# The expert stage of a fused embedding, attention and routed FFN kernel: rows of 64 experts by 2 units, gates loaded twice, gelu in place in PSUM

## The chip, the cores and the metric

The program runs on one core of a Trainium2 chip. The metric is the device time of one execution in microseconds (us). The engines are TensorE (PE; its weight loads are PEld), VectorE (DVE), ScalarE (ACT), GpSimd (POOL) and SyncE (SP, which here only issues DMAs). Each takes its own queue in order; semaphores tie them.

## What is computed

64 images give 16 patch tokens and 77 text tokens each, 5952 tokens of 192 numbers. After an attention of its own kind comes the part that the change is about, for each of S=8 subspaces of R=16 numbers, with M=64 experts of H=32 hidden units and the best K=4 chosen:

```
z = einsum('nd,sdr->nsr', layernorm(h), P)
scores = einsum('nsr,smr->nsm', z, C);  topv, topi = top_k(scores, 4);  w = softmax(topv)
hid = gelu(einsum('nsr,nskrh->nskh', z, W1[s,topi]) + b1[s,topi])      # tanh form
comb = einsum('nskr,nsk->nsr', einsum('nskh,nskhr->nskr', hid, W2[s,topi]) + b2[s,topi], w)
h = h + gelu(comb @ G1 + g1b) @ G2 + g2b
```

## The kernel before

Three stages follow each other. The **first** (to about 141 us) embeds: PE multiplies one-hots with the text tables and the patches with their matrix, POOL gathers word rows, DVE normalizes, SP stores the text rows (`store_text`, L426). Beside it W1 is split into three bf16 parts, W2 is placed into `w2p` by ACT, and each part of b2 into `b2p`.

The **second** (to about 858 us) goes through 16 units of 372 tokens with attention (a), its second half (b) and router (g) of three units interleaved in one pass (`pass_pe`, `pass_dve`, `pass_act`, `pass_pool`). It ends with the gates of all 512 experts for each token, zero where an expert isn't chosen, transposed by PE into PSUM. They are split into three bf16 parts: ACT casts (`gate_part1`), DVE subtracts (`rest`, L1143), ACT casts the rest (`gate_part2`), POOL subtracts again (`gate_part3`, L662). SP stores the three parts to DRAM. PE makes the product of gates and b2 (`bias`), ACT copies it.

The **third**, the expert stage, doesn't gather weights: it computes all experts for 12 tiles of TN=496 tokens and multiplies the hidden values by the gates. A tile has 8 blocks of 4 quads, 32 quads; a quad has 4 chunks k of 128 rows, each 16 experts by 8 units in a row of products. Its steps are `hidden` (PE, two bf16 products of 496 columns into one of two PSUM pairs, twice a quad), gelu of a pair by ACT into `hid` in SBUF (L936), `spread` (PE: the gates of 16 experts, spread over 128 rows by the 0/1 matrix `sel`, into one of two PSUM banks, L1561), the multiply of the whole quad by DVE into `gated` (L1326, 1984 elements), and `decode` (PE: 4 fp32 products into the four 32-row groups of one bank, summed over the tile, L1573). `gated` holds two blocks; `decode(block, k)` reads chunk k of all four quads of a block and runs one block later. POOL takes every eighth quad (`POOL_QUADS`, L740) from a copy of the gates that ACT makes. After a tile ACT copies the sum (L946), POOL adds the bias, and PE, ACT and DVE do G1, gelu, G2 and the last add (L1581, L950, L1589, L1338) inside the next tile. The order in each queue is written out by hand: `tile_pe` issues per quad the next spread, a hidden pair two quads ahead (`AHEAD` = 4 pairs), a decode, and another hidden pair. SP reloads gates and codes of the next tile by quarters (`refill`) and starts each tile with a load of the bias (L523).

## Time and profile before

| | |
|---|---|
| Time, median of 3 runs | 1804.54 us (1804.47 to 1810.88) |
| Span of the profiled execution | 1811.7 us |
| PE busy in the span | 1622.6 us (90%) |
| DVE, ACT, POOL busy | 1351.4, 1095.4, 718.0 us |
| First stage, to the last text store | about 141 us |
| Second stage, to the first expert gelu | about 717 us |
| Expert stage to its last decode | about 936 us, 12 tiles |

The times are those of whole executions; the span of the profiled one is 7.2 us over their median. Busy times overlap, so they don't add up to the span. A timeline row is an instruction, or some of the same kind merged (x), with its start and its length. What stands in brackets is the idle time of the engine before it, and what ended that. The records of matmuls overlap, since a matmul drains while the next one streams: the distance of two starts says what one costs in the queue, not its length.

### The profile page before, as it was taken

The page shows a single profiled execution, that of the slowest core. Times are in us where ns is not written, and L with a number is a line of the kernel's source. Part 1 is how long each engine was busy: PE and PEld are TensorE (multiplying, and loading weights), DVE is VectorE, ACT ScalarE, POOL GpSimd, SP SyncE. Part 2 cuts the span into 40 slices and gives each one's busy share as a digit, 9 for nine tenths or more (in the row PEclk, how much of TensorE's full clock was granted, in tenths as well). Part 3 has the DMA queues.
Part 4 walks back from the last instruction along what each step waited for, and adds up shares of the span by engine and source line. Part 5 has one row for each costly group of instructions (what it writes and reads, how often), then busy time and mean ns, then how long its engine had stood idle before and what let it go on. Part 6 is the DMA issues. An engine that isn't in the chain of part 4 may idle for free.

```text
span 1811.7 us, 31074 instructions
## 1 busy us (share of the span) xinstructions
PE 1622.6 (90%) x8824; PEld 674.4 (37%) x8824; DVE 1351.4 (75%) x2824; ACT 1095.4 (60%) x2122; POOL 718.0 (40%) x656
## 2 busy tenths in 40 slices
PE   5974888888888888874999999999999999999997
PEld 3631665555666665661122222222222212222221
DVE  4471488878888878875878877878878878878874
ACT  0131244545444445522888888888888888888884
POOL 4460366656666666663222222222222222222221
PEclk9755899989999999985899999999999999999998
DMA  7337012112112221114211121212212121121200
GB/s 225 99 92 85 22 42 80 57 55 65 55 55 58 72 77 56 58 50 112 51 26 43 38 51 25 66 32 48 49 25 56 30 56 40 39 51 25 66 24 9
DMA packets 120652, 102.38 MB, mean 57 GB/s; under 512 B 16951, under 2 KB 117743, under 8 KB 120175
## 3 DMA queue, kind: packets, MB, share of 16 engines
q1 hardware_dynamic: 117097, 94.99, 21.1%
q0 software_dynamic: 2112, 3.79, 0.8%
q10 hardware_dynamic: 1376, 2.88, 0.5%
q8 instruction: 21, 0.34, 0.1%
q14 instruction: 46, 0.38, 0.1%
HBM read 58.74 MB, written 39.62 MB: 54 GB/s over the span
## 4 chain that ended last, share of the span: by engine, by line
PE 73%; DVE 13%; issue 5%; POOL 3%; ACT 3%; DMA 2%; SPq 0%; DVEq 0%; POOLq 0%; ACTq 0%
PE pair L1546 22%; PE bank L1573 20%; PE bank L1561 6%; PE bank L1478 4%; PE pair L1447 4%; DVE arena L1118 3%; PE pair L1458 3%; PE pair L1417 2%; PE pair L1416 2%; DVE arena L1098 2%; PE bank L1366 2%; DVE arena L1107 2%; DVE arena L1201 1%; PE bank L1589 1%; PE bank L1440 1%
## 5 line engine op out<-in xcount | busy, mean ns | idle before, releaser
L1326 DVE TENSOR_TENSOR arena<-arena,bank 128x1984 f32<-128x1984 f32 x336 | 734.1, 2218 | 176.2 <-ACT arena L936 162.1
L936 ACT ACTIVATE arena<-pair 128x992 f32<-128x992 f32 x768 | 739.0, 998 | 156.7 <-PE pair L1546 156.7
L740 POOL TENSOR_TENSOR arena<-arena 128x992 f32<-128x992 f32 x96 | 219.1, 2304 | 698.0 <-PE bank L1573 685.0
L1546 PE MATMUL pair<-arena,w_stack 99*128 99x496 bf16 x1536 | 459.5, 382 | 13.6 <-ACT arena L936 13.6
L1573 PE MATMUL bank<-arena,w_pad 128*32 128x496 f32 x3072 | 399.0, 592 | 1.2 <-DVE arena L1326 1.2
L1546 PEld LDWEIGHTS pair<-arena,w_stack 99*128 99x128 bf16 x1536 | 88.1, 97 | 412.0 <-ACT arena L936 311.5
L1561 PE MATMUL bank<-arena,sel 48*128 48x496 bf16 x384 | 147.0, 383 | 0.6 <-ACT arena L838 0.6
L1573 PEld LDWEIGHTS bank<-arena,w_pad 128*32 128x32 f32 x3072 | 60.8, 108 | 160.4 <-issue 158.3
L1458 PE MATMUL pair<-arena 128*128 128x94 f32 x768 | 110.2, 306 | 2.6 <-DVE arena L1165 2.4
L1478 PE MATMUL bank<-arena 128*124 128x192 f32 x576 | 106.9, 337 | 3.7 <-POOL arena L675 3.7
L1458 PEld LDWEIGHTS pair<-arena 128*128 128x128 f32 x768 | 106.6, 222 | 3.3 <-DVE arena L1165 2.6
L667 POOL TENSOR_TENSOR arena<-arena 128x372 f32<-128x372 f32 x96 | 92.1, 974 | 33.1 <-DVE arena L1170 32.9
L1447 PE MATMUL pair<-arena 128*32 128x93 f32 x768 | 69.6, 302 | 36.8 <-DVE arena L1201 36.8
L1478 PEld LDWEIGHTS bank<-arena 128*124 128x124 f32 x576 | 94.4, 190 | 11.4 <-issue 5.5
L1561 PEld LDWEIGHTS bank<-arena,sel 48*128 48x128 bf16 x384 | 35.4, 92 | 161.2 <-issue 148.4
L1403 PE MATMUL bank<-ident,arena 124*128 124x124 f32 x96 | 25.0, 294 | 76.3 <-DVE arena L1098 76.3
L831 ACT ACTIVATE arena<-pair 128x93 f32<-128x93 f32 x384 | 91.4, 271 | 0.0
L1417 PE MATMUL pair<-arena 64*128 64x372 f32 x192 | 90.9, 556 | 0.0
L1416 PE MATMUL pair<-arena 128*128 128x372 f32 x192 | 86.9, 536 | 1.3 <-ACT arena L823 1.0
L822 ACT COPY arena<-bank 128x372 f32<-128x372 f32 x32 | 15.0, 468 | 116.9 <-PE bank L1404 116.9
L831 ACT ACTIVATION_READ_ACCUMULATOR arena<-pair 128x1 f32 x384 | 85.1, 230 | 0.0
L675 POOL TENSOR_TENSOR arena<-arena 128x372 f32<-128x372 f32 x96 | 81.1, 865 | 5.1 <-DVE arena L1188 5.1
(141 smaller groups left out, 1929.0 us busy)
## 6 DMA issues: line engine op xcount, KB each, us to landing
gate_parts<-arena SPq DMA_DIRECT2D x48, 372.0 KB, 6.7
arena<-gate_parts SPq DMA_DIRECT2D x576, 31.0 KB, 1.8
arena<-h_scratch SPq DMA_DIRECT2D x32, 279.0 KB
arena<-z_parts SPq DMA_DIRECT2D x144, 62.0 KB, 2.2
h_scratch<-arena SPq DMA_DIRECT2D x16, 279.0 KB
z_parts<-arena SPq DMA_DIRECT2D x48, 93.0 KB, 1.7
arena<-h_scratch SPq DMA_DIRECT2D x12, 372.0 KB
out_h<-arena SPq DMA_DIRECT2D x12, 372.0 KB
```

Source lines behind the costliest of these rows:

```text
L740: p_.tensor_tensor(gated[:, block % 2, j, pair], hid[:, quad % 4, pair], gcopy.unsqueeze(1).to_broadcast([128, 2, TN]), ALU.mult).then_inc ...
L831: last = a_.activation(wsq[:, c, N * b:N * b + N], src[:, N * b:N * b + N], ACT.Square, accum_out=n2[:, c, b:b + 1])
L936: a_.activation(hid[:, quad % 4, 2 * (pair % 2):2 * (pair % 2) + 2], (pair0, pair1)[pair % 2][:, :, 0:TN], ACT.Gelu_apprx_tanh).then_inc(s ...
L1326: v_.tensor_tensor(gated[:, block % 2, j], hid[:, quad % 4], gate_banks[quad % 2][:, 0:TN].unsqueeze(1).to_broadcast([128, KH, TN]), ALU.m ...
L1416: t_.matmul(o, wq0[:, 128 * c:128 * c + 128], xt0["A"], start=True, stop=False)
L1417: t_.matmul(o, wq1[:, 128 * c:128 * c + 128], xt1["A"], start=False, stop=True).then_inc(s_wp, 1)
L1447: last = t_.matmul(pair1[32 * b:32 * b + 32, 0, 0:N], lsel[:, b, c], wsq[:, c, N * b:N * b + N], start=(c == 0), stop=(c == CH - 1))
L1458: last = t_.matmul(pair0[:, c % 2, (N + 1) * b:(N + 1) * (b + 1)], headsel[:, b, c], pi, start=True, stop=True)
L1478: last = t_.matmul(o, wpi[:, c, ST * s:ST * s + ST], wout[:, c], start=(c == 0), stop=(c == CH - 1))
L1546: mm = t_.matmul((pair0, pair1)[pair % 2][:, a, 0:TN], w1s[:, x:x + 128], zst[:, o, j], start=True, stop=True)
L1561: t_.matmul(gate_banks[quad % 2][:, 0:TN], sel[rows], gst[rows, block, j // 2], start=True, stop=True).then_inc(s_gb, 1)
L1573: mm = t_.matmul(code_bank[32 * j:32 * j + 32, 0:TN], w2p[:, chunk(2 * j + o, eb, k)], gated[:, block % 2, j, k], start=(block == 0 and k ...
```

## The change

A product row of the expert stage holds 64 experts by 2 units instead of 16 by 8. A quad is split into two **duos** of two chunks, 64 duos per tile; a quad covers the 64 experts of one subspace with 8 of their units, a duo with 4 of them. So the 128 gate rows that multiply it are the 64 gates loaded twice, into partitions 0 to 63 and 64 to 127 of `gst` (fp32), straight from DRAM. `spread`, `sel` and its banks go; the two banks become `pair2`, the third PSUM pair of a ring. ACT's gelu of a duo writes back into its pair, and DVE multiplies from PSUM (992 elements, 42 duos of a tile). The 22 duos of `POOL_DUOS` have their gelu written into SBUF, where POOL multiplies them. A hidden product waits until the previous user of its pair is multiplied (or, for a POOL duo, until its gelu is done). The gates are kept in fp32 only, so in the second stage `gate_part2`, `gate_part3` and `rest` go and one copy stays; b2 is placed once in fp32 and `bias` has 4 products instead of 24. The weights are regrouped to the new rows: W2 comes in 32 small loads that SP issues after the last image product (`sp.wait_ge(s_ips, 8)`), between text stores 2 and 3; b1 in 8 loads; W1's casts and ACT's placing are cut into four and eight instructions.

```diff
-POOL_QUADS = [q for q in range(QUADS) if q % 8 == 4]
-DVE_QUADS = QUADS - len(POOL_QUADS)
+DUOS = 2 * QUADS
+POOL_DUOS = [d for d in range(DUOS) if d % 11 in (2, 5, 8, 10) and d != 32]
+DVE_DUOS = DUOS - len(POOL_DUOS)
+RING = [d % 3 for d in range(DUOS - 4)] + [0, 1, 0, 2]
 AHEAD = 4
+BIAS_AFTER = 10
...
+def dve_gated(tile, duo):
+
+    return DVE_DUOS * tile + sum(d not in POOL_DUOS for d in range(duo + 1))
+
+
+def pool_gated(tile, duo):
+
+    return len(POOL_DUOS) * tile + sum(d <= duo for d in POOL_DUOS)
+
+
+def same_buffer_before(tile, duo):
+
+    for d in range(duo - 1, -1, -1):
+        if RING[d] == RING[duo]:
+            return tile, d
+    return tile - 1, max(d for d in range(DUOS) if RING[d] == RING[duo])
+
+
+def first_of_half_block(duo, mine):
+
+    return not any(d in mine for d in range(duo - duo % 8 + duo % 2, duo, 2))
...
-        banks = [ctx.enter_context(nc.psum_tensor(f"bank{i}", [128, 512], F32)) for i in range(2)]
+        pair2 = ctx.enter_context(nc.psum_tensor("pair2", [128, 2, 512], F32))
+        banks = [pair2[:, 0], pair2[:, 1]]
...
-        gst = c3(128, [8, 2, TN], BF16)
+        gst = c3(128, [2, PAIRS, TN])
         zst = c3(ZROWS, [2, PAIRS, TN], BF16)
         assert c3.at <= attended_end
-        hid = c3(128, [4, KH, TN])
+        hid = c3(128, [2, 2, TN])
...
+            sp.wait_ge(s_ips, 8)
+            w2_from = t["w2"].rearrange("(m g a) (s e x) -> a e g m s x", m=16, a=2, s=S, e=EB)
+            for a in range(2):
+                for e in range(EB):
+                    for g in range(EB):
+                        rows = slice(64 * a + 16 * e, 64 * a + 16 * e + 16)
+                        sp.dma_start(w2f[rows, g], w2_from[a, e, g]).then_inc(s_w2f, 16)
...
-            def load_gates(tile, q):
-                for p in range(3):
-                    for a in range(2):
-                        for b in range(2):
-                            r = 64 * a + 16 * p
-                            sp.dma_start(gst[r:r + 16, 2 * q + b],
-                                         gq_r[p, a, q // 2, q % 2, b, :, :, bass.ds(tile * TN, TN)]
-                                         ).then_inc(s_gl[q], 16)
+            def load_gates(tile, o):
+                for h in range(2):
+                    sp.dma_start(gst[64 * h:64 * h + 64, o],
+                                 gq_r[o, :, :, bass.ds(tile * TN, TN)]).then_inc(s_gl[o], 16)
...
-                wait_apart(sp, (s_gb, QUADS * (tile - 1) + 8 * (q + 1)),
-                           (s_hp1, 2 * QUADS * (tile - 1) + 16 * (q + 1)))
-                load_gates(tile, q)
-                if q % 2 == 1:
-
-                    load_codes(tile, q // 2)
+            def refill(tile, o):
+
+
+                wait_apart(sp, (s_hp1, DUOS * (tile - 1) + DUOS // 2 * (o + 1)))
+                load_codes(tile, o)
+                last = DUOS // 2 * (o + 1) - 1
+                wait_apart(sp, (s_gat, dve_gated(tile - 1, last)), (s_pg, pool_gated(tile - 1, last)))
+                load_gates(tile, o)
...
-                if has(g - 1):
-                    gate_part3(g - 1, 2)
...
+            def gate_duo(tile, duo):
+
+                quad, a = divmod(duo, 2)
                 block, j = divmod(quad, PAIRS)
-                wait(pool, s_code, QUADS * tile + PAIRS * (block - 1))
-                pool.wait_ge(s_gc, pool_quads(tile, quad))
-                pool.wait_ge(s_hid, 2 * QUADS * tile + 2 * quad + 2)
-                for half in range(2):
-                    pair = slice(2 * half, 2 * half + 2)
-                    p_.tensor_tensor(gated[:, block % 2, j, pair], hid[:, quad % 4, pair],
-                                     gcopy.unsqueeze(1).to_broadcast([128, 2, TN]), ALU.mult).then_inc(s_pg, 1)
+                if duo == first_pool[block // EB]:
+                    pool.wait_ge(s_gl[block // EB], 32 * (tile + 1))
+                if first_of_half_block(duo, POOL_DUOS):
+                    wait(pool, s_code, QUADS * tile + PAIRS * (block - 2) + 2 * a + 2)
+                pool.wait_ge(s_hid, DUOS * tile + duo + 1)
+                p_.tensor_tensor(gated[:, block % 2, j, 2 * a:2 * a + 2], hid[:, POOL_DUOS.index(duo) % 2],
+                                 gst[:, block // EB, j].unsqueeze(1).to_broadcast([128, 2, TN]),
+                                 ALU.mult).then_inc(s_pg, 1)
...
+            def gates_copy(u, s):
                 act.wait_ge(s_gt, SUB * u + s + 1)
                 if s == 0:
-                    wait(act, s_gd, 48 * u)
+                    wait(act, s_gd, 16 * u)
                     wait(act, s_bp, u)
-                a_.copy(gh[:, 0, :, ST * s:ST * s + ST],
-                        gt_bank(s)[:, 0:4 * ST].rearrange("p (a b) -> p a b", a=4)).then_inc(s_g1, 1)
-
-            def gate_part2(u, s):
-                act.wait_ge(s_grr, SUB * u + s + 1)
-                a_.copy(gh[:, 1, :, ST * s:ST * s + ST], grr[:, s]).then_inc(s_g2, 1)
+                a_.copy(gh[:, :, ST * s:ST * s + ST],
+                        gt_bank(s)[:, 0:4 * ST].rearrange("p (a b) -> p a b", a=4)).then_inc(s_gc, 1)
...
+            def gelu(tile, duo):
+
+                act.wait_ge(s_hp1, DUOS * tile + duo + 1)
+                product = ring[RING[duo]][:, :, 0:TN]
+                if duo in POOL_DUOS:
+                    wait(act, s_pg, pool_gated(tile, duo) - 2)
+                    a_.activation(hid[:, POOL_DUOS.index(duo) % 2], product, ACT.Gelu_apprx_tanh).then_inc(s_hid, 1)
+                else:
+                    a_.activation(product, product, ACT.Gelu_apprx_tanh).then_inc(s_hid, 1)
...
-                if has(g - 1):
-                    rest(g - 1, 2)
...
+            dve_duos = [d for d in range(DUOS) if d not in POOL_DUOS]
+            first_dve = [min(d for d in dve_duos if d >= DUOS // 2 * o) for o in range(2)]
+
+            def gate_duo(tile, duo):
+                quad, a = divmod(duo, 2)
                 block, j = divmod(quad, PAIRS)
-                if j == 0 or quad - 1 in POOL_QUADS:
-                    wait(dve, s_code, QUADS * tile + PAIRS * (block - 1))
-                v_.tensor_tensor(gated[:, block % 2, j], hid[:, quad % 4],
-                                 gate_banks[quad % 2][:, 0:TN].unsqueeze(1).to_broadcast([128, KH, TN]),
+                if duo == first_dve[block // EB]:
+                    dve.wait_ge(s_gl[block // EB], 32 * (tile + 1))
+                if first_of_half_block(duo, dve_duos):
+                    wait(dve, s_code, QUADS * tile + PAIRS * (block - 2) + 2 * a + 2)
+                dve.wait_ge(s_hid, DUOS * tile + duo + 1)
+                v_.tensor_tensor(gated[:, block % 2, j, 2 * a:2 * a + 2], ring[RING[duo]][:, :, 0:TN],
+                                 gst[:, block // EB, j].unsqueeze(1).to_broadcast([128, 2, TN]),
                                  ALU.mult).then_inc(s_gat, 1)
...
-                for i in range(6):
-                    for j in range(PAIRS):
-                        mm = t_.matmul(pair1[32 * j:32 * j + 32, 0, 0:UT], b2p[:, j, WP[i]], gh[:, ZP[i], j],
-                                       start=(i == 0), stop=(i == 5), skip_group_check=True)
+                for j in range(PAIRS):
+                    mm = t_.matmul(pair1[32 * j:32 * j + 32, 0, 0:UT], b2p[:, j], gh[:, j], start=True, stop=True)
...
-            def hidden(tile, pair):
-
-                block, j = divmod(pair // 2, PAIRS)
-                o, eb = divmod(block, EB)
-                if pair % QUADS == 0:
+            def hidden(tile, duo):
+
+                quad, a = divmod(duo, 2)
+                block, j = divmod(quad, PAIRS)
+                o, hb = divmod(block, EB)
+                if duo % (DUOS // 2) == 0:
                     pe.wait_ge(s_zl[o], 96 * (tile + 1))
-                wait(pe, s_hid, 2 * QUADS * tile + pair - 1)
-                for a in range(2):
-                    x = chunk(2 * j + o, eb, 2 * (pair % 2) + a) * 128
-                    mm = t_.matmul((pair0, pair1)[pair % 2][:, a, 0:TN], w1s[:, x:x + 128], zst[:, o, j],
+                before = same_buffer_before(tile, duo)
+                if before[1] in POOL_DUOS:
+                    wait(pe, s_hid, DUOS * before[0] + before[1] + 1)
+                else:
+                    wait(pe, s_gat, dve_gated(*before))
+                for k in range(2):
+                    x = chunk(2 * j + o, hb, 2 * a + k) * 128
+                    mm = t_.matmul(ring[RING[duo]][:, k, 0:TN], w1s[:, x:x + 128], zst[:, o, j],
                                    start=True, stop=True)
                 mm.then_inc(s_hp1, 1)
 
-            def spread(tile, quad):
-
-                block, j = divmod(quad, PAIRS)
-                if quad % (QUADS // 4) == 0:
-                    pe.wait_ge(s_gl[block // 2], 192 * (tile + 1))
-                before = (tile, quad - 2) if quad >= 2 else (tile - 1, quad - 2 + QUADS)
-                if before[1] in POOL_QUADS:
-                    pe.wait_ge(s_gc, pool_quads(*before))
-                else:
-                    wait(pe, s_gat, dve_gated(*before))
-                rows = slice(64 * (j % 2), 64 * (j % 2) + 48)
-                t_.matmul(gate_banks[quad % 2][:, 0:TN], sel[rows], gst[rows, block, j // 2],
-                          start=True, stop=True).then_inc(s_gb, 1)
-
             def decode(tile, block, k):
 
-                if k == 0:
-                    pe.wait_ge(s_gat, dve_gated(tile, PAIRS * block + PAIRS - 1))
-                    wait(pe, s_pg, 2 * pool_quads(tile, PAIRS * block + PAIRS - 1))
-                    if block == 0:
-                        wait(pe, s_comb, tile)
+                if k % 2 == 0:
+                    needed = 2 * (PAIRS * block + PAIRS - 1) + k // 2
+                    pe.wait_ge(s_gat, dve_gated(tile, needed))
+                    pe.wait_ge(s_pg, pool_gated(tile, needed))
+                if k == 0 and block == 0:
+                    wait(pe, s_comb, tile)
...
                 for quad in range(QUADS):
-                    spread_next(quad)
                     hidden_ahead(quad, AHEAD)
+                    hidden_ahead(quad, AHEAD + 1)
                     decode_next(quad)
-                    hidden_ahead(quad, AHEAD + 1)
```

PE inside a tile, around the output product of the tile before. In the rows `pair` is a hidden product, `sel` a spread, `w_pad` a decode. Before:

```order
L1573 MATMUL bank<-arena,w_pad 32x496 x4
L1546 MATMUL pair<-arena,w_stack 128x496 [waits hidden_gelu]
L1546 MATMUL pair<-arena,w_stack 128x496
L1561 MATMUL bank<-arena,sel 128x496 [waits hidden_gated]
L1546 MATMUL pair<-arena,w_stack 128x496 [waits hidden_gelu]
L1546 MATMUL pair<-arena,w_stack 128x496
L1573 MATMUL bank<-arena,w_pad 32x496 [waits hidden_gated_by_pool,hidden_gated]
L1573 MATMUL bank<-arena,w_pad 32x496 x3
L1546 MATMUL pair<-arena,w_stack 128x496 [waits hidden_gelu]
L1546 MATMUL pair<-arena,w_stack 128x496
L1561 MATMUL bank<-arena,sel 128x496 [waits gates_copied]
```

After, from decode k=3 of block 0 to decode k=0 of block 1 (register rows compute what is waited for):

```order
L1528 MATMUL bank<-arena,w_pad 32x496 x4
L83 REGISTER_ALU
L1514 MATMUL pair<-arena,w_stack 128x496 [waits hidden_gated]
L1514 MATMUL pair<-arena,w_stack 128x496
L83 REGISTER_ALU
L1514 MATMUL pair<-arena,w_stack 128x496 [waits hidden_gated]
L1514 MATMUL pair<-arena,w_stack 128x496
L1523 REGISTER_ALU [waits hidden_gated]
L1528 MATMUL bank<-arena,w_pad 32x496 [waits hidden_gated_by_pool]
L1528 MATMUL bank<-arena,w_pad 32x496 x3
```

The spread is gone, both hidden products of a quad stand ahead of its decode, and they wait for a multiply (`hidden_gated`) where they waited for a gelu.

DVE, first tile of the expert stage, the multiplies before (`chunk_decoded` is the semaphore of the decodes):

```order
L1326 TENSOR_TENSOR arena<-arena,bank 128x1984 [waits bias_stored,gates_stored,hidden_gelu,z_stored,gates_spread,h1_stored,w1_stack_written]
L1326 TENSOR_TENSOR arena<-arena,bank 128x1984 [waits gates_spread,hidden_gelu] x6
L1326 TENSOR_TENSOR arena<-arena,bank 128x1984 [waits chunk_decoded,gates_spread,hidden_gelu]
L1326 TENSOR_TENSOR arena<-arena,bank 128x1984 [waits gates_spread,hidden_gelu] x3
L1326 TENSOR_TENSOR arena<-arena,bank 128x1984 [waits chunk_decoded,gates_spread,hidden_gelu]
L1326 TENSOR_TENSOR arena<-arena,bank 128x1984 [waits gates_spread,hidden_gelu] x2
```

And after:

```order
L1291 TENSOR_TENSOR arena<-pair,arena 128x992 [waits bias_stored,gates_stored,gates_loaded0,z_stored,hidden_gelu,h1_stored,w1_stack_written]
L1291 TENSOR_TENSOR arena<-pair,arena 128x992 [waits hidden_gelu] x10
L1291 TENSOR_TENSOR arena<-pair,arena 128x992 [waits hidden_gelu,chunk_decoded] x2
L1291 TENSOR_TENSOR arena<-pair,arena 128x992 [waits hidden_gelu] x3
L1291 TENSOR_TENSOR arena<-pair,arena 128x992 [waits hidden_gelu,chunk_decoded] x2
L1291 TENSOR_TENSOR arena<-pair,arena 128x992 [waits hidden_gelu] x3
```

The twelfth and thirteenth multiply (duos 17 and 18) wait for decodes of two blocks before; 16, 19 and 21 are POOL's.

POOL in a pass of the second stage, before:

```order
L635 TENSOR_SCALAR arena<-arena 124x3 [waits normed_G,moments_G]
L637 TENSOR_TENSOR arena<-arena 124x3 [waits var_eps_G]
L667 TENSOR_TENSOR arena<-arena 128x372 [waits w_pi] x2
L662 TENSOR_TENSOR arena<-arena 128x4x124 [waits gate_part2]
L667 TENSOR_TENSOR arena<-arena 128x372 [waits w_pi] x4
L641 TENSOR_TENSOR arena<-arena 128x372 [waits z_part1]
```

And after:

```order
L647 TENSOR_SCALAR arena<-arena 124x3 [waits normed_G,moments_G]
L649 TENSOR_TENSOR arena<-arena 124x3 [waits var_eps_G]
L674 TENSOR_TENSOR arena<-arena 128x372 [waits w_pi] x6
L653 TENSOR_TENSOR arena<-arena 128x372 [waits z_part1]
```

The residue of the gates (L662) that stood behind the first two products with `w_pi` is gone.

## Rows read from the trace of the kernel before

**Rows 1.** Stretches of the execution: us, busy us of each engine (x instructions), granted clock, DMA share.
```profile
870.00:1750.00 880.00, 871.66 (x4818) 190.07 (x4816) 701.24 (x338) 727.13 (x793) 223.07 (x103) 1.00 0.18 41
588.00:592.00 4.00, 1.91 (x17) 1.91 (x17) 4.00 (x10) 0.83 (x2) 3.35 (x4) 0.97 0.26 78
592.00:596.00 4.00, 4.00 (x12) 2.43 (x12) 2.95 (x9) 0.03 (x1) 2.42 (x3) 0.60 0.57 183
```

**Rows 2.** Costliest groups of the page: busy us, mean ns of one | idle before, releaser.
```profile
L1326 DVE TENSOR_TENSOR arena<-arena,bank 128x1984 f32<-128x1984 f32 x336 | 734.1, 2218 | 176.2 <-ACT arena L936 162.1
L936 ACT ACTIVATE arena<-pair 128x992 f32<-128x992 f32 x768 | 739.0, 998 | 156.7 <-PE pair L1546 156.7
L740 POOL TENSOR_TENSOR arena<-arena 128x992 f32<-128x992 f32 x96 | 219.1, 2304 | 698.0 <-PE bank L1573 685.0
L1546 PE MATMUL pair<-arena,w_stack 99*128 99x496 bf16 x1536 | 459.5, 382 | 13.6 <-ACT arena L936 13.6
L1573 PE MATMUL bank<-arena,w_pad 128*32 128x496 f32 x3072 | 399.0, 592 | 1.2 <-DVE arena L1326 1.2
```

**Rows 3.** Timeline of one quad: start us, us, engine line; all engines.
```profile
1299.97 0.59 PE L1546 MATMUL pair<-arena,w_stack 99*128 99x496 bf16 x2
1300.49 0.38 PE L1561 MATMUL bank<-arena,sel 48*128 48x496 bf16 x1
1300.59 1.91 ACT L936 ACTIVATE arena<-pair 128x992 f32<-128x992 f32 x2 [0.42 <-PE pair L1546]
1301.32 1.04 PE L1573 MATMUL bank<-arena,w_pad 128*32 128x496 f32 x8
1302.30 0.38 PE L1546 MATMUL pair<-arena,w_stack 99*128 99x496 bf16 x1
```

**Rows 4.** Timeline of SP, bias loads of two tiles that follow each other.
```profile
1341.23 0.34 SPq L523 DMA_DIRECT2D arena<-bias_codes  x1
...
1418.91 0.36 SPq L523 DMA_DIRECT2D arena<-bias_codes  x1
```

**Rows 5.** Timeline, end of the expert stage.
```profile
1783.95 6.88 DVE L1326 TENSOR_TENSOR arena<-arena,bank 128x1984 f32<-128x1984 f32 x3 [2.13 <-ACT arena L936]
1790.89 3.53 PE L1573 MATMUL bank<-arena,w_pad 128*32 128x496 f32 x32 [1.23 <-DVE arena L1326]
1794.49 0.57 ACT L946 COPY arena<-bank 128x496 f32<-128x496 f32 x1 [5.91 <-PE bank L1573]
1800.58 0.56 DVE L1338 TENSOR_TENSOR arena<-bank,arena 124x384 f32<-124x384 f32 x1 [9.74 <-PE bank L1589]
```

**Rows 6.** Timeline, a multiply that waited for its gelu.
```profile
1365.20 1.00 ACT L936 ACTIVATE arena<-pair 128x992 f32<-128x992 f32 x1
1366.19 6.48 DVE L1326 TENSOR_TENSOR arena<-arena,bank 128x1984 f32<-128x1984 f32 x3 [1.28 <-ACT arena L936]
```

**Rows 7.** Stage before: POOL's timeline; L1098 in two stretches (ns min/median/max); PE's timeline.
```profile
588.85 1.07 POOL L662 TENSOR_TENSOR arena<-arena 128x496 bf16<-128x496 f32 x1
...
L1098 DVE TENSOR_SCALAR arena<-arena x1: 1115/1115/1115, 588.9 to 588.9; 124x192 f32<-124x192 f32 x1
...
L1098 DVE TENSOR_SCALAR arena<-arena x3: 369/370/882, 580.8 to 581.8; 124x192 f32<-124x192 f32 x3
...
590.09 0.33 PE L1403 MATMUL bank<-ident,arena 124*128 124x124 f32 x1 [2.46 <-DVE arena L1098]
```

**Rows 8.** Timeline of POOL where the expert stage begins.
```profile
848.16 1.06 POOL L662 TENSOR_TENSOR arena<-arena 128x496 bf16<-128x496 f32 x1 [0.76 <-ACT arena L876]
...
856.38 0.50 POOL L730 MEMSET arena<- 1x496 f32 x1 [7.17 <-DMA bias_codes<-arena]
```

**Rows 9.** First stage: ACT's timeline, DVE's timeline, SP's text stores (ns min/median/max).
```profile
84.17 0.32 ACT L768 COPY arena<-bank 128x192 f32<-128x192 f32 x1 [4.03 <-PE bank L1368]
...
105.74 0.94 DVE L1009 TENSOR_TENSOR arena<-arena 112x768 f32<-112x768 f32 x1
...
L426 SPq DMA_DIRECT2D h_scratch<-arena x44: 553/566/832, 40.9 to 138.8; - x44
```

235 lines of the change are left out of this document (80 added, 155 removed).

## The prediction

> **What bounds the kernel now.** I read the busy times by stretch first. In the expert stage PE is busy 871.7 of 880 us at the full clock [rows 1], while ACT is busy 83%, DVE 80% and POOL 25% of it. So it is bound by the matmul queue, with nothing to gain on the others. The period of a tile, from one bias load to the next in SP's timeline, is 77.68 us [rows 4]: twelve such tiles make half of the time. The timeline of one quad [rows 3] shows what fills it: a pair of hidden products takes 0.52 us until the next group starts (1299.97 to 1300.49), the spread product 0.31, the second pair again 0.52 (so it began at 1300.80), four decode products 0.98 (1301.32 to 1302.30), together 2.33. 32 quads are 74.6 us; the remaining 3.1 us of a tile are the output products. ACT waits 0.42 us per quad for PE there.
>
> The stage before (attention, router and gates; 160 to 850 us) is bound by a chain that passes through DVE and PE in turns. One link of it [rows 7]: the third of the normalizations (L1098) takes 1.115 us while POOL does a residue of the gates (L662, 588.85 to 589.92), and PE waits 2.46 us for them; with POOL idle the same instruction takes 0.37 us.
>
> **The change, expert stage: PE's work.** Per quad the spread product goes (0.31), and the two pairs now stand side by side, which saves one more changeover: 0.52 - 0.413 = 0.11. That leaves 2.33 - 0.42 = 1.91 us, and 32 x 1.91 + 3.1 = 64.2 us per tile. If PE stayed the bound, 13.5 us per tile or 162 us in all would be gained. The other engines would allow about that: ACT 64 gelus at 0.91 us from start to start (two in 1.91, the second 1.00, [rows 3]) = 58.2 plus 1.2 for code copy and output gelu; DVE 42 multiplies at 1.10 and two adds = 47; POOL 22 at 2.25 to 2.30 = 51 [rows 2].
>
> **What the ring costs.** A hidden product goes into one of three PSUM pairs, and for 42 of 64 duos the pair is held until DVE has multiplied. Before, a pair was free after its gelu. One turn costs: hidden start to gelu start 0.62 (1299.97 to 1300.59, [rows 3]); gelu 1.00 [rows 2]; gelu end to DVE start 0.00 (1365.20 + 1.00 against 1366.19, [rows 6]); multiply 1.19; DVE end to PE start 0.06 (1783.95 + 6.88 = 1790.83 against 1790.89, [rows 5]). The multiply of 992 elements isn't in the trace: it lies between 0.56 us for 384 elements [rows 5] and 2.22 for 1984 [rows 2], both with one operand in PSUM, so 0.56 + 608 x 1.04 ns = 1.19; consecutive ones overlap by 0.09 (three in 6.48, [rows 6]), so 1.10 from start to start. The turn is 2.87 us for a distance of three duos, where PE needs 0.96 per duo. PE takes its queue in order, and a decode stands behind every two hidden products. So an even duo, its multiply, the odd duo three further, then a decode: 2.87 + 0.52 + 0.98 = 4.37 us for two quads, where PE alone would need 3.82. With a second gelu and multiply in between (+0.91 + 1.10) it is 6.38 for three quads (5.73 alone).
>
> **A second wait, on the gated buffer.** Duo 8b+1 (units 2 and 3 of the block) writes what decode k=3 of block b-2 reads. That decode stands in PE's queue behind hidden 8b+3; hidden 8b+4 needs multiply 8b+1. So in blocks 2 to 4, where 8b+1 and 8b+2 are DVE's: decode start to its semaphore 1.08 (1.04 to the end of its records, [rows 3], and 0.04 for the last step, 0.07 at most between PE's end 1794.42 and the copy at 1794.49, [rows 5]), multiply 1.10, multiply and release 1.25, hidden and changeover 0.52: 3.95 us for one quad instead of 1.91.
>
> **One tile added up** (32 quads, along PE, ACT and DVE in turn): blocks 2 to 4 with the buffer wait 3 x 3.95 + 0.47 for an output add between = 12.3 (3 quads); four two-quad loops 17.5 and 1.7 for output products in them = 19.2 (8); two three-quad loops 12.8 (6); the four quads over the tile's boundary 0.98 + 4.88 + 2.87 + 0.52 = 9.25; duo 1 behind decode k=3 of block 6, 1.08 + 1.25 + 2.87 + 0.52 = 5.7 (2); the code copy, which ACT does before gelu 10 and which waits for the last decode: 1.08 + 0.48 + 0.91 + 1.00 + 1.10 + 1.25 + 0.52 = 6.3 (2); seven quads at 1.91 = 13.4. Sum 78.9 us, 1.25 more than now, with PE idle 15 us of it. **12 tiles: +15 us.**
>
> Bounds of the unknown durations. No row has a gelu that writes PSUM. From below, 0.91 us, its present distance from start to start, gives 77.7 per tile, no change in all; from above, the 1.19 us of DVE's operation of that size out of PSUM gives 82.5, +58. I take the 0.998 of the same gelu into SBUF, the nearest row [rows 2]; a twentieth more, 1.05, would be +24. A multiply of 1.15 or 1.22 gives 78.1 or 79.5, +5 to +22. The POOL multiplies have their row.
>
> On the gelu in PSUM the Trainium skill speaks to both sides ("ScalarE: Activation LUTs", section "Step-by-step: what each stage is for"): an activation into PSUM is faster than into SBUF, with the caveat that this is only of use where TensorE doesn't need most of PSUM. It gives no figure, and no run here yet shows either; by its first half the sum would move toward the lower bound, and the ring above is a case of its caveat.
>
> Ends of the stage. First gelu to last decode is now 1794.4 - 858.4 = 936.0 us, 12 x 77.68 and 3.9 more, part of it slow clock in the first tile. In the new order the first tile has no earlier tile to wait for (-2.8), the slow clock stays (some +4): **-2.5 us.** The gate loads (two for each half of a tile) have half a tile, 39 us, to land, and cost nothing; without that cover the first multiply of a half would wait for all of one landing.
>
> **The stage before.** POOL's residue (48 L662), DVE's subtraction (48 L1143) and ACT's second cast go. DVE's and ACT's lie in slots where the next step waits for another engine, so nothing is taken for them. POOL's third one lies on the link in question [rows 7]: 1.115 - 0.37 = 0.75 us per unit, with 15 of 16 units **-11 us**; what is late next is PE's transposes, that follow at once. Bounds 0 (if POOL's next product slides into the gap) and -13. The bias product gets shorter off the chain. **The hand-over** loses one cast, one subtraction, one residue and most of the bias product of the last unit: POOL ends the residue at 849.22, and the store lands at 856.38 [rows 8]; copied gates would be ready some 3 us earlier, with one larger store: **-3**, bounds -4.5 and 0.
>
> These stretched rows have their rule in the Trainium skill ("SBUF — State Buffer", section "Who interferes with whom"): one port pair is shared by DVE and GpSimd as an exclusive lock, taken by a tensor_scalar in its fast mode and not by a tensor_tensor with a single SBUF input. The trace agrees, 1.115 against 0.37 us, and by the rule the new multiplies with one PSUM input stay free of POOL's 22.
>
> **First stage.** SP now waits for the last image product (its copy is at 84.17, [rows 9]) and then issues 32 small loads of w2, before the store of text step 3. At 0.566 us per issue (L426) that is 18.1 us, to 102.6; the store follows to 104.9 and lands near 107. DVE's step at 105.74 needs it: **+2 us**, bounds 0 and +8 (if small rows land slowly, the gathers and ACT's placing of w2 come late as well). Behind SP's wait stand only these stores.
>
> **Sum.** +15 - 2.5 - 11 - 3 + 2 = +0.5 us on the profiled span of 1811.7, which is 7 us over the median of 1804.5; what lies around the span doesn't change. On the median: **1805 us.** Half a per cent (9 us) is about what a measurement can tell.
>
> **Rivals.**
> *A: the ring doesn't bind.* For it: PE alone needs 64.2, every engine has room. Against: [rows 3, 5, 6] give each link of the turn, and PE's queue is in order. Time 1804.5 - 162 - 12 = 1630. Chance 0.06.
> *B: links are shorter.* Gelu in PSUM at 0.91 us, multiply at 1.15: 76.8 per tile, -10 instead of +15: 1780; half of that 1792. For it: gelus already follow each other at 0.91. Against: the 1.19 interpolates between two rows. Chance 0.23.
> *C: slower, PE's clock falls.* In the stage before, a stretch of 4 us with 1.9 us of PE work is followed by one at 0.60 of the clock [rows 1], between 1.2 and 2.4 GHz. In the new stage PE is idle 15 of 79 us, in pieces up to 1.3 us, instead of 1 in 80. If each tile spends 5 us at the lower clock, 2.5 us are lost: +30, 1835. It decides from one such stretch of 3 us per tile on. Against it: the pieces are short and PE is 80% busy. Chance 0.16.
> *D: the early loads or the unchanged pass eat the gain of the first two stages:* +13 to +19, 1820. Chance 0.13.
> *Forecast* as summed, 1796 to 1813: 0.42.
>
> **Range and chances.** 1780 to 1838 leaves out A and the ends of C. Faster by over 0.5%: A, B = 0.29; within 0.5%: 0.42; slower: C, D = 0.29.
>
> **What would show it.** In the new profile: the tile period 78.9; PE idle near 15 us per tile, waiting for ACT and DVE's multiply; PE waits 1.2 to 1.3 us behind each decode k=3 of blocks 0 to 2, with DVE waiting for PE's decode; gelus at 1.00; multiplies at 1.19; the third L1098 at 0.4 us; text stores held up behind the w2 loads. A period near 64 would prove the ring wrong, a granted clock under 0.98 in the expert stage would be C, a gelu row of 0.9 B.

## The result: slower by 2.2%, 1845 us where 1805 was forecast

| | before | after |
|---|---|---|
| median, us | 1806.8 (1804.5 to 1810.9) | 1845.0 (1839.2 to 1853.0) |
| ratio, 95% interval | | 1.022 (1.018 to 1.026) |
| profiled execution: span, us | 1811.7 | 1851.2 |
| mean granted clock of PE | 0.920 | 0.903 |

Times are medians; one of the four executions of e9 (5431.7 us) and one of e10 (1766.0 us), both slow ones, are left out of theirs. The time lies above the range (1780 to 1838). Split at the first h0 load of the attention stage (SP's first load from `h_scratch`) and at the first gelu of the expert stage, the profiled span grew by +6.4 us in the first stage (forecast +2), by -27.9 in the attention stage with the hand-over (forecast -14), and by +61.5 in the expert stage up to its last decode (forecast +12.5). So the miss of 40 us is, to 1 us, the sum of +49 in the expert stage, +4 in the first and -14 in the attention stage: without that last one the forecast would have been further off.

The expert stage by stretches, kernel after (us, busy us of PE, PEld, DVE, ACT, POOL, granted clock, DMA share); the first line answers to the first of [rows 1], the others are one place of a tile:

```profile
870.00:1750.00 880.00, 737.88 (x4180) 164.25 (x4180) 526.88 (x467) 656.67 (x701) 544.18 (x244) 0.96 0.21 46
...
1286.00:1288.00 2.00, 0.81 (x3) 0.25 (x4) 1.86 (x4) 0.98 (x1) 1.71 (x1) 0.88 0.00 0
1288.00:1290.00 2.00, 2.00 (x10) 0.20 (x8) 1.22 (x2) 0.98 (x1) 0.00 (x0) 0.50 0.00 0
1290.00:1292.00 2.00, 2.00 (x12) 0.49 (x12) 1.03 (x1) 0.59 (x1) 0.00 (x0) 0.77 0.00 0
```

PE stands much of 1286 to 1288, and then has work for 4 us, part of which it does at the lower of its two levels (1.2 GHz, shown as 0.50). This comes twice a tile; "dip" below means such a stretch. The costliest groups of the page, which answer to [rows 2] (count | busy us, mean ns of one | idle before, releaser):

```profile
L1291 DVE TENSOR_TENSOR arena<-pair,arena 128x992 f32<-128x992 f32 x504 | 584.5, 1187 | 376.6 <-ACT pair L929 261.7
L742 POOL TENSOR_TENSOR arena<-arena 128x992 f32<-128x992 f32 x264 | 602.9, 2296 | 381.3 <-ACT arena L927 338.9
L929 ACT ACTIVATE pair<-pair 128x992 f32<-128x992 f32 x504 | 488.3, 983 | 151.7 <-PE pair L1514 143.8
L1514 PE MATMUL pair<-arena,w_stack 99*128 99x496 bf16 x1536 | 435.7, 393 | 162.4 <-DVE arena L1291 161.4
L1528 PE MATMUL bank<-arena,w_pad 128*32 128x496 f32 x3072 | 418.3, 619 | 0.0
```

SP's timeline, bias loads of two tiles that follow each other, as [rows 4]:

```profile
1268.58 0.36 SPq L544 DMA_DIRECT2D arena<-bias_codes  x1
1351.33 0.36 SPq L544 DMA_DIRECT2D arena<-bias_codes  x1
```

The operations cost what the forecast took (multiply 1.187 us, gelu in PSUM 0.983, POOL's multiply 2.30), but the tile takes 82.75 us here and 83.2 on average, not 78.9. The decode product has a mean of 619 ns where it had 592.

PE's timeline at that place shows the waits that the forecast had priced as the second wait on the gated buffer (0.56 and 0.97 us), and behind them the low clock: two hidden products take 1.01 us where the two ahead of them take 0.59, and the decode of eight records 1.88 us where it takes 1.04 elsewhere. The last two rows are the second such place of the tile, four quads later, with a wait of 1.41 us where the forecast had 1.2 to 1.3:

```profile
1284.74 0.91 PE L1544 MATMUL bank<-g2w,arena 65*124 65x192 f32 x4
1286.21 0.59 PE L1514 MATMUL pair<-arena,w_stack 99*128 99x496 bf16 x2 [0.56 <-DVE arena L1291]
1287.78 1.01 PE L1514 MATMUL pair<-arena,w_stack 99*128 99x496 bf16 x2 [0.97 <-DVE arena L1291]
1288.71 1.88 PE L1528 MATMUL bank<-arena,w_pad 128*32 128x496 f32 x8
...
1299.34 0.59 PE L1514 MATMUL pair<-arena,w_stack 99*128 99x496 bf16 x2 [1.41 <-DVE arena L1291]
1300.96 1.74 PE L1528 MATMUL bank<-arena,w_pad 128*32 128x496 f32 x8
```

### The profile page after: what moved, and what is told of

Its sections match the earlier page's. It is cut to its first block, busy times and chain, and to the rows that moved or that the text cites. A ratio compares the mean times of both kernels' runs of the same rounds, so it can differ in the third digit from the quotient of the medians.

```text
span 1851.2 us, 28150 instructions
## 1 busy us (share of the span) xinstructions
PE 1522.0 (82%) x8184; PEld 646.2 (35%) x8184; DVE 1158.1 (63%) x2942; ACT 1042.4 (56%) x2031; POOL 1046.4 (57%) x770
## 4 chain that ended last, share of the span: by engine, by line
PE 48%; DVE 23%; issue 12%; ACT 10%; POOL 3%; DMA 2%; SPq 1%; DVEq 1%; ACTq 0%; POOLq 0%
DVE arena L1291 12%; PE pair L1514 12%; PE bank L1528 12%; ACT pair L929 6%; PE pair L1410 4%; PE bank L1441 3%; DVE arena L1093 3%; PE pair L1382 3%; PE pair L1381 2%; PE pair L1421 2%; PE pair L1331 2%; ACT arena L927 2%; DVE arena L1073 1%; PE bank L1403 1%; DVE arena L1082 1%
## 5 line engine op out<-in xcount | busy, mean ns | idle before, releaser
L1291 DVE TENSOR_TENSOR arena<-pair,arena 128x992 f32<-128x992 f32 x504 | 584.5, 1187 | 376.6 <-ACT pair L929 261.7
L742 POOL TENSOR_TENSOR arena<-arena 128x992 f32<-128x992 f32 x264 | 602.9, 2296 | 381.3 <-ACT arena L927 338.9
L929 ACT ACTIVATE pair<-pair 128x992 f32<-128x992 f32 x504 | 488.3, 983 | 151.7 <-PE pair L1514 143.8
L1514 PE MATMUL pair<-arena,w_stack 99*128 99x496 bf16 x1536 | 435.7, 393 | 162.4 <-DVE arena L1291 161.4
L1528 PE MATMUL bank<-arena,w_pad 128*32 128x496 f32 x3072 | 418.3, 619 | 0.0
L1514 PEld LDWEIGHTS pair<-arena,w_stack 99*128 99x128 bf16 x1536 | 109.2, 99 | 616.7 <-DVE arena L1291 428.7
L927 ACT ACTIVATE arena<-pair 128x992 f32<-128x992 f32 x264 | 263.1, 997 | 66.6 <-PE pair L1514 61.3
L674 POOL TENSOR_TENSOR arena<-arena 128x372 f32<-128x372 f32 x96 | 91.9, 976 | 28.3 <-DVE arena L1137 27.9
L668 POOL TENSOR_TENSOR arena<-arena 124x512 f32<-124x512 f32 x48 | 56.1, 1168 | 59.5 <-DVE arena L1112 58.8
L1410 PEld LDWEIGHTS pair<-arena 128*32 128x32 f32 x768 | 70.6, 146 | 44.2 <-DVE arena L1168 44.2
```

What stands on the lines that cost most here:

```text
L742: p_.tensor_tensor(gated[:, block % 2, j, 2 * a:2 * a + 2], hid[:, POOL_DUOS.index(duo) % 2], gst[:, block // EB, j].unsqueeze(1).to_broad ...
L927: a_.activation(hid[:, POOL_DUOS.index(duo) % 2], product, ACT.Gelu_apprx_tanh).then_inc(s_hid, 1)
L929: a_.activation(product, product, ACT.Gelu_apprx_tanh).then_inc(s_hid, 1)
L1291: v_.tensor_tensor(gated[:, block % 2, j, 2 * a:2 * a + 2], ring[RING[duo]][:, :, 0:TN], gst[:, block // EB, j].unsqueeze(1).to_broadcast( ...
L1410: last = t_.matmul(pair1[32 * b:32 * b + 32, 0, 0:N], lsel[:, b, c], wsq[:, c, N * b:N * b + N], start=(c == 0), stop=(c == CH - 1))
L1514: mm = t_.matmul(ring[RING[duo]][:, k, 0:TN], w1s[:, x:x + 128], zst[:, o, j], start=True, stop=True)
```

## The experiments on the expert stage

All are edits of the changed kernel. Each was timed beside the kernel before, on the same chip, and its ratio is to that; the changed kernel itself was not timed again, so a difference in us to its 1845 is one between sets of runs, in which the kernel before had medians of 1805 to 1812. In the diffs "..." marks what is left out. Two theories stood at the start: the missing 4.3 us a tile are lost to the granted clock behind PE's waits, or the links of the loops are longer than they were taken.

**e1: PE has work in its waits.** Products that change nothing, at the places of the long waits.

```diff
+FILL = {0: (5, 0), 8: (5, 2), 12: (2, 4), 16: (5, 2), 30: (4, 0)}
...
+            def fill(quad, ahead):
+                for _ in range(FILL.get(quad, (0, 0))[ahead - AHEAD]):
+                    t_.matmul(code_bank[:, 0:128], zeros, ident[:], start=False, stop=False, skip_group_check=True)
...
                 def hidden_ahead(quad, ahead):
                     duo = 2 * quad + ahead
+                    fill(quad, ahead)
```

> The changed kernel with 23 small products a tile (128 by 128, zeros times the identity, added to the code's sums, so that nothing changes in them) put into PE's queue where PE stands longest for a ring pair: ahead of the hidden products of quads 0, 8, 12, 16 and 30. Nothing else is moved. Theory 1 (the clock): the changed kernel's tile of 83.2 us is the forecast's 78.9 of loops and second waits, and the other 4.3 are lost while the granted clock of TensorE is at its lower level, twice a tile, just behind these waits (1286 to 1292 and 1300 to 1306 us in its trace, where windows of 2 us show 0.50 to 0.88). With PE busy through them the clock stays at 1.00, and the tile takes 79 to 80 us although PE has more to do: 12 tiles of 4 us off 1845, about 1795 to 1800. Theory 2 (longer hand-offs): the 4.3 us are in the loops themselves, the low clock costs nothing because PE isn't the bound; then the clock rises and the tile stays at 83 us or grows by the products' own time: 1845 to 1860.

Measured: 1810.0 us, ratio to before 1.001 (0.998 to 1.004). By the table it is 29 products a tile, not 23. The stretch:

```profile
870.00:1690.00 820.00, 755.44 (x4638) 231.64 (x4642) 510.12 (x453) 634.52 (x678) 526.89 (x236) 1.00 0.22 48
```

and two bias loads of SP:

```profile
1241.81 0.36 SPq L546 DMA_DIRECT2D arena<-bias_codes  x1
1321.73 0.36 SPq L546 DMA_DIRECT2D arena<-bias_codes  x1
```

The clock is 1.00 in this stretch, a tile takes 79.9 us here and 80.0 on average, with more work for PE. 83.2 - 80.0 = 3.2 us a tile, 12 x 3.2 = 38 us; the medians differ by 35, and the profiled expert stage, first gelu to last decode, fell from 997.5 to 961.5 us. Theory 1 holds in kind, with three quarters of its size: 1795 to 1800 was expected. What is left, 80.0 against 78.9, isn't the products' own cost, for ahead of quads 12 and 16 the decodes follow each other at 4.53 and 4.07 us in e1, and at 4.53 and 4.06 in e12, which has none there; and the changed kernel's 83.2 less two dips, at their price in e2 below, is 80.1 too. So the forecast's sum of loops and waits was 1.1 us a tile too short.

**e12: the control.** The same number of products at quads where PE waits little; the edit is shown against e1.

```diff
-FILL = {0: (5, 0), 8: (5, 2), 12: (2, 4), 16: (5, 2), 30: (4, 0)}
+FILL = {18: (5, 0), 20: (5, 0), 22: (5, 0), 24: (7, 0), 26: (7, 0)}
```

> A control for e1: the same 29 small products a tile, but ahead of the hidden products of quads 18, 20, 22, 24 and 26, where PE waits little, and none at the long waits of quads 0, 8, 12, 16 and 30. Theory 1 (the clock falls behind each long wait, and what counts is that PE has work in it): the two dips of some 4 us a tile stay (mean granted clock 0.95 to 0.97 in the expert stage), and the tile is 83 us or somewhat more, time 1845 to 1870. Theory 2 (the products help by making PE busier on the whole): clock 1.00 and 80 us a tile as in e1, 1810.

Measured: 1926 us in a single execution, where 1845 to 1870 was expected, a tile 88 to 91 us:

```profile
870.00:1690.00 820.00, 699.39 (x4114) 204.97 (x4115) 452.16 (x402) 562.46 (x600) 466.56 (x209) 0.96 0.19 41
```

The clock stays at 0.96 and the two dips stay, as theory 1 has it. The products cost 7 us a tile here (90.1 on average against 83.2), which I had not priced; in e1 they cost nothing that shows. By itself this doesn't refute theory 2, since the longer tile keeps PE at 85% busy, where it had 84% in the changed kernel and 92% in e1. But e2 and e5 below speak against it: PE is 87% busy in e2 at a mean clock of 0.99, and 88% busy in e5, with one wait of 6.2 us a tile, at 0.96.

**e2: a third slot for the gated chunks.**

```diff
+SLOT = [0, 1, 2, 0, 1, 2, 0, 1]
+BACK = [2, 2, 5, 3, 3, 3, 3, 3]
...
-        gated = c3(128, [2, PAIRS, KH, TN])
+        gated = c3(128, [3, PAIRS, KH, TN])
...
-    wait(dve, s_code, QUADS * tile + PAIRS * (block - 2) + 2 * a + 2)
+    wait(dve, s_code, QUADS * tile + PAIRS * (block - BACK[block]) + 2 * a + 2)
```

(the same for GpSimd, and SLOT[block] for block % 2 in the decode.)

> The changed kernel with a third slot for the gated chunks (blocks 0 to 7 of a tile in slots 0, 1, 2, 0, 1, 2, 0, 1), so that a block's first multiplies wait for decodes three blocks back, long done, in place of two. Theory 1 (second wait on the gated buffer, as forecast): the waits of up to 1.4 us of PE that follow it at quads 8, 12 and 16 go, which is 3.4 us a tile by the forecast's loops, and the low clock behind them goes with them (about 4 us): tile 75.5 to 77 us, time 1845 - 12 x 7 = about 1760. Theory 2 (the ring alone makes all waits, the buffer is free in time anyway): tile 83 us, 1845.

Measured: 1773.8 us, ratio 0.982 (0.977 to 0.988). The stretch:

```profile
870.00:1690.00 820.00, 711.60 (x4172) 161.03 (x4168) 522.01 (x464) 652.79 (x697) 545.46 (x244) 0.99 0.22 49
```

and VectorE's waits in it, for PE's output product and for decodes (line waited for: us in total, times, longest):

```profile
DVE arena L1305 <- PE bank L1546: 41.5, 20, 3.2
DVE arena L1293 <- PE bank L1530: 25.9, 10, 2.6
```

In the changed kernel the multiplies waited 78.8 us for decodes in this stretch, here 25.9; the clock is at 0.99. Of ten tiles seven take 78.1 to 78.3 us and three 76.6 to 76.7. One of each, as two loads of the bias and two more:

```profile
1152.80 0.36 SPq L546 DMA_DIRECT2D arena<-bias_codes  x1
1229.47 0.36 SPq L546 DMA_DIRECT2D arena<-bias_codes  x1
...
1382.69 0.36 SPq L546 DMA_DIRECT2D arena<-bias_codes  x1
1460.84 0.36 SPq L546 DMA_DIRECT2D arena<-bias_codes  x1
```

In stretches of 2 us each of the seven has one dip, and the three have none. So one kernel shows the price of a dip by itself, 1.55 us, and two of them are the 3.2 us of e1. The three tiles also give the price of the second wait: 80.0 - 76.6 = 3.4 us, as expected. Theory 1 holds, but not all dips went with the waits, and so the mean tile of 77.7 us lies over the 75.5 to 77 expected, and the time 14 us over 1760. VectorE also stands 2.1 us at each of 20 output adds (in the changed kernel nine of them waited, 2.9 us each); no run shows whether that costs time.

**e3: decode first in each quad.**

```diff
                 for quad in range(QUADS):
+                    decode_next(quad)
                     hidden_ahead(quad, AHEAD)
                     hidden_ahead(quad, AHEAD + 1)
-                    decode_next(quad)
```

> The changed kernel with PE's order in a quad turned: decode, then the two pairs of hidden products, in place of hidden, hidden, decode. The decode for which a block's multiplies wait then no longer stands behind a hidden product that itself waits for a ring pair. By the forecast's loops (turn of a ring pair 2.87 us, PE alone 64.2 us a tile) the second wait goes and the decode lies in the shadow of the gelu and the multiply: 72 us a tile, clock 1.00, 1845 - 12 x 11 = about 1710. Rival: the decode of an even chunk waits for a multiply that is only just done (it is asked for one step earlier), PE then waits at the decode in place of the hidden products, and the ring stays as full as it was: tile 80 to 84 us, 1800 to 1850.

Measured: 1717.2 us, ratio 0.951 (0.946 to 0.957). The tile takes 72.3 us, the clock is 1.00. The stretch:

```profile
870.00:1690.00 820.00, 749.03 (x4472) 172.09 (x4469) 563.47 (x500) 701.20 (x749) 586.38 (x262) 1.00 0.23 50
```

The longest of VectorE's waits in it, for its gelu; none of its multiplies waits for a decode:

```profile
DVE arena L1291 <- ACT pair L929: 249.3, 286, 2.4
```

One line in another place is worth 128 us, 35 to 38 of them by the clock (e1), the rest by the waits. The loops foretold it (72 us a tile, about 1710 us); the rival, that PE would wait at the decode instead, doesn't hold: PE waits 3.5 us at decodes in 820.

**e6: decode first, 26 duos on GpSimd.**

```diff
-POOL_DUOS = [d for d in range(DUOS) if d % 11 in (2, 5, 8, 10) and d != 32]
+POOL_DUOS = [d for d in range(DUOS) if d % 10 in (0, 3, 6, 8)]
```

> The kernel e3 (decode first in each quad) with 26 duos of a tile on GpSimd (duos whose last digit is 0, 3, 6 or 8) in place of 22, so that two duos in five free their pair after the gelu. In e3 the tile takes 72.4 us, of which PE waits 8 for VectorE's multiplies. Theory 1 (the turn of pairs held by VectorE still sets it): fewer of them in a row, by the same loops 68.7 us a tile, 1717 - 12 x 3.6 = about 1673; GpSimd's 26 x 2.30 = 59.8 us and its bias add fit. Rival (GpSimd becomes the bound: 61 of 69 us busy in an order of its own, with two buffers only): the ring waits for GpSimd at the gelu, 73 us or more a tile, 1720 or more.

Measured: 1680.0 us, ratio 0.930 (0.925 to 0.936), where about 1673 was expected, a tile 69.25 us: within 0.6 us of theory 1. GpSimd is busy 688 of 800 us (870 to 1670), and its multiplies wait only for their gelu.

**e4: VectorE's gelus to SBUF, the pair free at once.**

```diff
-                if before[1] in POOL_DUOS:
-                    wait(pe, s_hid, DUOS * before[0] + before[1] + 1)
-                else:
-                    wait(pe, s_gat, dve_gated(*before))
+                wait(pe, s_hid, DUOS * before[0] + before[1] + 1)
...
-                    a_.activation(product, product, ACT.Gelu_apprx_tanh).then_inc(s_hid, 1)
+                    wait(act, s_gat, dve_gated(tile, duo) - HIDV)
+                    a_.activation(hidv[:, (dve_gated(0, duo) - 1) % HIDV], product, ACT.Gelu_apprx_tanh).then_inc(s_hid, 1)
...
-                v_.tensor_tensor(gated[...], ring[RING[duo]][:, :, 0:TN],
+                v_.tensor_tensor(gated[...], hidv[:, (dve_gated(0, duo) - 1) % HIDV],
```

> The changed kernel with the gelu of VectorE's duos written to three buffers in SBUF in place of back into the ring pair in PSUM; VectorE multiplies from there, and the pair is free when the gelu is done, as for GpSimd's duos. Theory 1 (what costs is how long the pair is held: 2.87 us a turn, of which 1.19 are the multiply): the turn falls to 1.7 us, three pairs feed PE without a wait, and the tile is PE's own 64 to 65 us at clock 1.00: 1845 - 12 x 18.5 = about 1620 to 1630. Rival 1 (two engines on SBUF): VectorE's multiply with both operands in SBUF and GpSimd's 2.30 us multiply hinder each other; GpSimd's 22 multiplies at 3.0 us make 68 us a tile: about 1665. At 3.5 us 79 us a tile: about 1795. Rival 2 (the pair's holding isn't the bound): tile 83 us, 1845.

Measured: 1986.5 us, ratio 1.100 (1.093 to 1.106). The costliest groups of 870 to 1690 us:

```profile
L1294 DVE TENSOR_TENSOR arena<-arena 128x992 f32<-128x992 f32 x367 | 806.3, 2268 | 11.2 <-ACT arena L932 9.8 <-PE bank L1528 1.4
L744 POOL TENSOR_TENSOR arena<-arena 128x992 f32<-128x992 f32 x191 | 547.3, 2880 | 257.6 <-ACT arena L929 181.8 <-PE bank L1528 59.1 <-ACT arena L932 16.5
```

Neither theory 1 nor rival 1's prices hold. The engines do hinder each other, but VectorE pays most: its multiply goes from 1.19 to 2.27 us, 42 of them are 95 us, and that is the tile (94.7 us). So this kernel says nothing for or against the holding of the pair; it shows what the operand in PSUM was good for.

**e5: the same with all multiplies on VectorE,** and with four buffers for its gelus where e4 has three.

```diff
-POOL_DUOS = [d for d in range(DUOS) if d % 11 in (2, 5, 8, 10) and d != 32]
+POOL_DUOS = []
...
+HIDV = 4
...
```

> The kernel e4 (gelu of every duo into SBUF) with all 64 multiplies of a tile on VectorE and none on GpSimd (which only adds the bias). In e4 VectorE's multiply from two SBUF operands took 2.27 us (1.19 from PSUM and SBUF) and GpSimd's 2.88 (2.30). Theory 1 (GpSimd at work makes VectorE's multiply long): alone, VectorE's multiply of 992 elements takes 1.1 to 1.2 us again; 64 of them from start to start of 1.1 us make 70 to 73 us a tile, and the time is near 1845 - 12 x 11 = 1710. Theory 2 (two SBUF operands are slow in themselves): the multiply stays at 2.2 us or so, 64 of them make 140 us a tile, and the time is about 2500.

Measured: 1795.9 us in a single execution, where about 1710 was expected, a tile 78.6 us. The same groups, of 870 to 1670 us, and the stretch:

```profile
L1291 DVE TENSOR_TENSOR arena<-arena 128x992 f32<-128x992 f32 x654 | 725.1, 1194 | 68.6 <-ACT arena L929 56.6 <-PE bank L1524 12.0
L751 POOL TENSOR_TENSOR arena<-arena 128x496 f32<-128x496 f32 x10 | 163.4, 16338 | 642.6 <-ACT arena L933 642.6
...
870.00:1670.00 800.00, 701.18 (x4022) 155.62 (x4014) 731.40 (x674) 652.48 (x674) 163.38 (x10) 0.96 0.22 48
```

and PE's wait for the bias add, in total, times, longest:

```profile
PE bank L1532 <- POOL arena L751: 62.2, 10, 6.2
```

The multiply is at 1.19 us again, so theory 1 holds, and two operands in SBUF aren't slow in themselves. What I had not foreseen: GpSimd's only operation, an add of 496 elements that takes 1.26 us in the changed kernel, takes 16.3 us beside VectorE's unbroken multiplies, and PE waits 6.2 us a tile for it. The two in one tile, timeline of 1300 to 1345 us:

```profile
1299.66 28.75 DVE L1291 TENSOR_TENSOR arena<-arena 128x992 f32<-128x992 f32 x26
1333.55 2.29 DVE L1291 TENSOR_TENSOR arena<-arena 128x992 f32<-128x992 f32 x2 [5.14 <-ACT arena L929]
```

The add starts at 1313.16 and ends at 1329.50, 1.09 us after VectorE's last multiply (1328.41), which is less than its own 1.26. So it seems to get nothing done until VectorE stops, and VectorE stops only because PE, at the product that needs the add, gives it no more to multiply: the 16.3 us are no cost of the add, but the time until the others run dry. Less those 6.2 us the tile would be at 72.4, within what was expected; no run shows it.

## The experiments on the stages before

**e7: GpSimd's residue put back,** as a dead operation.

```diff
...
+            def residue(u, s):
+                pool.wait_ge(s_gc, SUB * u + s + 1)
+                p_.tensor_tensor(grr[:, s], gh[:, :, ST * s:ST * s + ST], gh[:, :, ST * s:ST * s + ST],
+                                 ALU.subtract).then_inc(s_g3, 1)
...
```

> The changed kernel with one dead operation put back into its second stage: GpSimd subtracts the copied gates from themselves (128x496, fp32, the three places of the pass at which it took the residue of the gates before), and nothing reads the result. The second stage and hand-over took 717.5 us before and 689.6 after, -27.9 where -14 was forecast; a pass 40.4 and 38.1. Theory 1 (forecast's mechanism: GpSimd's residue stretches VectorE's normalizations beside it): a pass takes 39 to 39.5 us and the stage 16 to 20 us more than in the changed kernel, the third normalizations are at 0.9 to 1.1 us again. Theory 2 (VectorE's own subtractions, 3 x 0.66 us a pass, were on the chain and not in slots of waiting): a pass stays at 38.1 to 38.4 us, the stage at 690 to 694.

Measured: 1870.0 us in a single execution, and from the first h0 load to the first gelu 721.7 us, against 682.2 to 697.1 in the nine kernels without it (after, e1 to e6, e8, e12) and 717.5 before. That is 32 us over the changed kernel, where 16 to 20 was expected, and as far as one profile tells, this operation alone gives back all of the gain. Short passes take 38.8 us as before, and 38.05 without it. One long pass of e7 in the timeline: VectorE's normalizations, GpSimd beside them, PE's wait:

```profile
459.77 2.86 DVE L1088 TENSOR_SCALAR arena<-arena 124x192 f32<-124x192 f32 x3 [0.97 <-POOL arena L652]
461.49 1.02 POOL L677 TENSOR_TENSOR arena<-arena 128x496 f32<-128x496 f32 x1
462.69 0.33 PE L1383 MATMUL pair<-ident,arena 124*128 124x124 f32 x1 [2.40 <-DVE arena L1088]
```

and the stretches of e7 from that wait on:

```profile
460.00:464.00 4.00, 1.60 (x13) 1.44 (x13) 4.00 (x8) 0.42 (x2) 3.35 (x4) 0.94 0.25 69
464.00:468.00 4.00, 4.00 (x16) 3.04 (x15) 2.29 (x8) 0.41 (x2) 2.53 (x4) 0.50 0.45 154
468.00:472.00 4.00, 4.00 (x7) 1.50 (x6) 1.96 (x6) 0.84 (x2) 1.71 (x3) 0.50 0.44 156
```

The same place in the timeline of the kernel after, which answers to [rows 7]:

```profile
577.15 2.16 DVE L1073 TENSOR_SCALAR arena<-arena 124x192 f32<-124x192 f32 x3 [0.98 <-POOL arena L649]
...
579.37 0.33 PE L1368 MATMUL pair<-ident,arena 124*128 124x124 f32 x1 [1.71 <-DVE arena L1073]
```

The three normalizations go from 2.92 us to 2.16, PE's wait from 2.46 to 1.71: the 0.75 us of the forecast, 11 us in all. The rest of the gain is the clock again: behind the longer wait it fell in more passes, or for longer. Before, of 15 passes six took 40.3 to 40.5 us and one 45.4; after, four took 39.4 to 39.7; in e7 four took 45.3. The size of this part is uncertain: a second profile of the kernel before (e11, below) is 11 us longer in this stage, by other long passes.

**e9: PE has work in the waits of the attention stage** (on e6).

```diff
+            def fill(n):
+                for _ in range(n):
+                    t_.matmul(banks[3][:, 384:512], ident[:], ident[:], start=True, stop=True)
...
                 if has(g):
+                    pe.wait_ge(s_h1, g + 1)
+                    fill(7)
                     transposes("G", g, (s_xt_["A"], a + 1) if has(a) else gates_read)
...
                 if has(a):
+                    fill(9)
                     logits(a)
```

> The kernel e6 with small products (identity by identity, 128 columns, into the unused columns of a PSUM bank) put into PE's queue in the attention stage: seven ahead of the transposes that wait for VectorE's normalizations of h1, nine ahead of the logits. In the changed kernel most passes of that stage take 38.1 us and every third or fourth 39.6 (in the residue kernel 38.8 and 45.3); in the long ones the granted clock is at 0.50 to 0.74 just behind the first of these waits. Theory 1 (these passes are long by the clock alone): all passes 38.0 to 38.3 us, the stretch from the first h0 load to the first gelu, 682 to 697 us in seven kernels with the same code, falls to 675 to 682; the time from 1680 to about 1673. Theory 2 (the long passes come from something else, a transfer or the queue of another engine): every third or fourth pass stays at 39.6, and the products make all passes longer where PE isn't waiting: 1680 to 1690.

Measured: 1651.7 us, ratio 0.913 (0.907 to 0.920), 28 us less than e6, where 7 was expected; the stage took 655.1 us, 29 less than in e6, where 675 to 682 was expected. From the fourth on every pass takes 36.4 to 36.5 us: not only the long ones had a stretch of low clock. In the kernel after, the logits of one pass in PE's timeline, with the wait ahead of them:

```profile
563.80 4.76 PE L1410 MATMUL pair<-arena 128*32 128x93 f32 x48 [2.61 <-DVE arena L1168]
```

two stretches there, still of after:

```profile
562.00:564.00 2.00, 0.20 (x2) 0.20 (x3) 2.00 (x7) 0.00 (x0) 1.04 (x1) 0.97 0.00 0
564.00:566.00 2.00, 2.00 (x19) 2.00 (x18) 2.00 (x9) 0.00 (x0) 0.00 (x0) 0.50 0.00 0
```

and the logits in e9, 1.6 us shorter:

```profile
580.13 3.16 PE L1410 MATMUL pair<-arena 128*32 128x93 f32 x48 [0.57 <-DVE arena L1168]
```

**e8 and e10: SP's loads of w2 in four groups** between the text stores, in the changed kernel and in e9.

```diff
             sp.wait_ge(s_ips, 8)
... (the 32 loads and the loop over store_text go)
+            load_w2(0)
+            for k in range(4):
+                store_text(k + 3, (k + 1) % 2)
+                if k < 3:
+                    load_w2(8 * k + 8)
...
```

> The changed kernel with SP's 32 loads of w2 in four groups of eight, one ahead of each of the text stores 3 to 6, in place of all 32 ahead of store 3. The first load of the attention stage was issued at 147.31 us after and 140.96 before, +6.35 where +2 was forecast. Theory 1 (the 16.7 us of issues in one piece hold up the store of text step 3 and VectorE's step for 5.9 us): each store is held up by 4.2 us at most, less than a text step takes, and the first load of the next stage comes at 141 to 143 us. Theory 2 (the transfers themselves, the strided casts or subtractions, 4.2 against 1.9 us on ACT and 4.0 against 2.3 us on VectorE, cost the time): it stays at 145 to 148 us. The expert stage is the changed kernel's.

> The kernel e9 with SP's loads of w2 in groups of eight between the text stores, as in e8. From the last image copy to the first h0 load of the attention stage it was 56.8 us before, 63.8 to 64.9 in eight kernels with the loads in one piece and 58.1 in e8, while the image copy itself came anywhere from 70.6 to 84.2 us. Theory 1 (the loads in one piece cost 6 to 7 us of the first stage, hidden in the profile by the scatter of the image products): 57 to 59 us again, and 6 us less time than e9, about 1667. Theory 2 (e8's stretch was short by chance): 64 us, no change against e9.

**e11: the kernel before, once more.**

> The kernel before, unchanged, for a second profile. Question: how far do its stages scatter from one execution to another? Theory 1 (the stretches that depend on no clock repeat): last image copy to first h0 load 56 to 58 us, short passes of the attention stage 38.8 us and third normalization at 1.1 us, tile period 77.7 us. Where the clock falls differs: the last image copy comes between 70 and 84 us, and the number of attention passes at 40.4 us instead of 38.8 is between 3 and 9. Theory 2: the difference of the stretches between the kernels before and after is itself scatter, and lies within what this kernel shows twice.

The first stage can't be read from one profile of each: the last image copy came at 84.17 us before (79.77 in e11), 83.42 after, and between 70.59 and 80.45 us in the kernels e1 to e7 with the same first stage. From that copy to the first h0 load the stretches repeat: 56.8 us before and in e11, 63.8 to 64.9 in the ten kernels with the loads in one piece, 58.1 in e8 and 57.8 in e10. ACT's last image copy and SP's first h0 load in the timeline of after:

```profile
83.42 0.32 ACT L773 COPY arena<-pair 128x192 f32<-128x192 f32 x1 [4.21 <-PE pair L1333]
147.31 0.27 SPq L466 DMA_DIRECT2D arena<-h_scratch  x1
```

of e8:

```profile
76.05 0.32 ACT L780 COPY arena<-pair 128x192 f32<-128x192 f32 x1 [2.35 <-PE pair L1340]
134.12 0.27 SPq L473 DMA_DIRECT2D arena<-h_scratch  x1
```

and of e11:

```profile
79.77 0.32 ACT L768 COPY arena<-bank 128x192 f32<-128x192 f32 x1 [2.35 <-PE bank L1368]
136.52 0.28 SPq L438 DMA_DIRECT2D arena<-h_scratch  x1
```

So the loads in one piece cost 7 us and four groups give back 6 of them; theory 1 of e8 and of e10 holds. (e8's first h0 load came at 134.12 us, below the 141 to 143 expected, because its image copy was early; its time of 1837.5 in a single execution says nothing by itself.) e10 measured 1642.4 us, ratio 0.908 (0.901 to 0.914), 9 us less than e9 where 6 were expected (in the profiles the image copy came 2.7 us earlier than in e9, which is of the scatter above). It is the best version: **9.2% less than the kernel before.** e11 took 1818.8 us in a single execution, its attention stage 728.9 us (717.5 in the first profile), its tile 77.7 both times; the short passes are 38.8 us again, five others take 40.3 to 40.4 and four 42.4 to 45.4. Its theory 1 holds. The difference of 28 us between before and after in that stage is more than this scatter of 11.

## Why the prediction was wrong, point by point

- **The ring and the loops: right, 1.1 us a tile short.** Multiply 1.187 us (taken 1.19), gelu in PSUM 0.983 (taken 0.998), sum 78.9 us a tile. e1 measured 80.0 with the clock up; e3 and e6 measured 72.3 and 69.25 where the same loops give 72 and 68.7. Which term is short isn't known. "The ring doesn't bind" and "links are shorter" are out.
- **The second wait on the gated buffer: right,** shown by e2: without it a tile is 3.4 us shorter, as the loops give. e3, with its decode ahead of the hidden products, fits.
- **The term that failed: PE's clock in the expert stage.** The sum took every product at its duration in the kernel before, at clock 1.00, though it had PE idle for 15 of 79 us. The clock's fall stood in the sum at nothing. It was rival C, at 0.16, and sized 5 us a tile at the lower clock, 2.5 us lost; e1 gives 83.2 - 80.0 = 3.2 us a tile, and the tiles of e2 with and without a dip give 1.55 a dip. That is 38 us of the 49 that the expert stage is over its forecast; 13 more are the 1.1 us a tile above, and its ends give 2 back. What I set against it, that the pieces are short and PE is 80% busy, fell: both dips of a tile stand behind waits that I had listed, at quads 12 (0.56 and 0.97 us) and 16 (1.41 and 0.50). A wait of that length is not always followed by one: in e2 one of 1.52 us was (tile from 1382.69), and one of 1.49 at the same place of the tile from 1152.80 was not. What decides between the two stays open.
- **The ends of the expert stage: about right,** 61.5 - 12 x 5.5 = -4.5 us for -2.5, the 5.5 being 83.2 - 77.7.
- **The attention stage: mechanism right, forecast at half its size.** 0.75 us a pass as forecast; the passes that lost the clock less often, 10 us, weren't counted, though [rows 1] showed one of them (0.60 at 592 to 596). The hand-over, from the start of the last logits to the first gelu, gave 6.1 us where 3 was forecast; e7, with the residue back, has 80.9 us there against 79.7 after and 85.8 before, so most of it is not the residue. Which of the casts, subtractions and products it is wasn't tried.
- **The first stage: mechanism right, 7 for 2 us,** within the bounds of 0 to 8. SP issues the 32 loads from 83.41 to 100.15 us, 16.7 us where 18.1 was taken, but the step held up is one earlier than I took, and waits 5.9 us:

```profile
100.63 7.23 SPq L447 DMA_DIRECT2D h_scratch<-arena  x9
105.14 0.96 DVE L993 TENSOR_TENSOR arena<-arena 112x768 f32<-112x768 f32 x1 [5.89 <-DMA h_scratch<-arena]
```

- **Early loads or the pass eat the gain (rival D): out,** the first two stages together gave 21.5 us where 12 was forecast. This was not foreseen, and it hid part of the miss.

## What to carry to other kernels

A sum along a chain, with durations from a trace at full clock, is safe where the new order leaves PE no waits: where it makes PE wait, look for low clock behind waits of the same length elsewhere in the same trace, and price them. The cheap test and cure are products that change nothing, put just into the waits (35 us here, 28 in the attention stage); elsewhere they cost their time. And where an engine's queue is in order, ask what stands ahead of the operation that frees a buffer: the decode in front of two hidden products instead of behind them was worth 128 us.

## What the runs showed of the hardware

- **VectorE and GpSimd on SBUF.** A multiply of 992 fp32 elements takes VectorE 1.19 us with one operand in PSUM, GpSimd at work or not (1.178 to 1.194 over 504 of them), and 1.19 with both in SBUF and GpSimd at rest (e5); with both in SBUF and GpSimd multiplying, 2.27 (e4). GpSimd's goes from 2.30 to 2.88, and its add of 1.26 to 16.3 us where VectorE doesn't rest for the first 15.2 of them. The Trainium skill has the rule ("SBUF — State Buffer", section "Who interferes with whom": an operation of VectorE with two SBUF inputs contends with one of GpSimd that reads SBUF, one with a single SBUF input doesn't). The traces agree on both halves; the sizes are the traces'.
- **PE's clock also falls without a wait.** In the first stage of the kernel after PE was busy for the whole of 24 to 58 us. Up to 45 us two of its image products take 0.98 us (the rows show a clock of 1.00 there, but these are the durations that go with 0.50 later on, so the rows can't be trusted that early). From 45.5 they take 0.58 us, and from 48.5 on 0.98 again, with no wait in between: the two stretches below. In e1, with the same code there, they take 0.58 from 42 to 73 us. This is the scatter of the image products, and no run here explains it. Stretches of the kernel after:

```profile
46.00:52.00 6.00, 6.00 (x20) 3.88 (x20) 1.55 (x4) 1.49 (x4) 4.59 (x6) 0.71 0.19 50
52.00:58.00 6.00, 6.00 (x18) 5.13 (x18) 3.92 (x15) 0.32 (x1) 2.52 (x4) 0.50 0.20 57
```

- **A gelu into PSUM** takes 0.983 us, into SBUF 0.997, for 992 elements: the Trainium skill ("ScalarE: Activation LUTs", section "Step-by-step: what each stage is for") says that an activation into PSUM is faster than into SBUF; the traces agree, by 14 ns.
